# Layer 0: the last of four weights-by-values products moved into the next body, the third one's sum at the body's end

## The chip, the cores and the metric

The kernel runs on one core of a Trainium2 chip. Its engines are TensorE (PE in the profile), VectorE (DVE), ScalarE (ACT), GpSimd (POOL) and SyncE (SP), which here only issues transfers. The metric is the device time of one execution in microseconds. The kernel before took 2502.35 us, the median of three runs (2502.28 to 2506.46).

## The reference

Two transformer layers over x of 16 sequences (batches), 256 tokens, 256 features, all in float32. Layer 0, cut to what matters here:

```python
# cross attention: 16 heads of 64, causal and key mask
x1 = x + tanh(g_xattn[0]) * xattn(layernorm(x), ctx)
# "mix": attention of each token over its own 16 heads of 16
n  = layernorm(x1);  h = rmsnorm(n, gamma1)
q  = h @ Wq + bq
k, v = split((h @ Wdown + bdown) @ Wup + bup)
att = softmax(einsum('bthd,btgd->bthg', q, k) / 4)   # per token, 16 x 16
o  = einsum('bthg,btgd->bthd', att, v)
y  = n + (o @ Wo + bo)
# "moe": 8 experts, all of them, weighted by a softmax gate
h2 = rmsnorm(y, gamma2)
gate = softmax(h2 @ Wg + bg)
x2 = x1 + tanh(g_ffn[0]) * (y + sum_e gate[e] * (h2 @ We[e]))
```

Layer 1 is a cross attention with 16 heads of 16 and a feed-forward part with a shared expert and two routed ones of 1024 hidden features. The change doesn't touch it.

## The kernel before

**Staging.** Layer 0 is a pipeline over the batches. `body(a, b, c, nxt)` works on four of them at once: the attention of batch a, the mix of batch b = a - 1, the moe of batch c = a - 2, and the first projections for nxt = a + 1. In a full body all four are there: bodies 2 to 14, of which 3 to 14 are a hardware loop. Bodies 0 and 1 fill the pipeline, bodies 15, 16 and 17 empty it. Body 16 runs beside layer 1's first body and body 17 beside its second: `side_by_side` merges the programs of the two layers on each engine by the numbers that they yield. Within layer 0 alone a yielded number sets no time; the order of the code does.

**Steps.** A body has STEPS = 20 steps. In step s PE writes the scores of heads s and s + 1 (every other step), transposes the probabilities of head s - 3, and multiplies with the values five steps late. DVE takes the masked maximum of head s (`attn_max`, L745) and the reciprocal of the sum of head s - 1 (`attn_sum`, L751), ACT the exponential and the scaling. Each engine works through its instructions in order and waits on semaphores. Beside the heads lie the other stages, given to steps by tables (`mix_at`, `expert_at`, `add_at`, `score_at`, `gather_at`, L221 to L226). They share the two PSUM banks `l0_side` in one fixed order of uses. The projections of a and nxt use the two banks `l0_attn`.

**The mix of batch b.** At the start of the body DVE finishes x1 of the last batch (`attn_final`, L753; L757 and L761), takes its variance (L587 to L592) and normalises it to n (L623). Two small powers on POOL (`power`, L337) give the inverse roots. `mix_rms` (L633) makes h. PE transposes h, and projects q, down, up0 and up1 in steps 2 to 6; DVE adds the biases (L639, L645, L651). Then POOL forms the products of queries and keys, 128 x 2048 elements each, in four pieces (`query_key`, L371), and DVE sums each over its 16 features (`mix_scores`, L655). After the fourth sum comes the softmax (L662 to L672, the exponential on ACT). Then POOL forms the four products of weights and values (`weigh`, L385) and DVE sums them (`mix_gather`, L678) into o. The buffer `prod` holds two pieces: piece k + 2 waits for the sum of piece k.

**The moe of batch c.** It begins at the start of the next body: PE waits for the fourth sum, transposes o (use "oT" of the side banks), ACT and DVE split the result into a high and a low part, PE multiplies with Wo ("out"), DVE adds bias and n (`moe_residual`, L685, L688). Step 1 has `moe_squares` (L695 to L700), step 2 `moe_normalise` (L706), step 4 the transposes of h2, step 5 the gate, steps 6 to 17 the eight experts on PE and their eight weighted additions on DVE (L729). Then x2 is stored.

**For nxt**, POOL splits the context (L344, L346), DVE takes the variance of x in step 3 and normalises it to xn in step 7 (L601); PE transposes xn in step 10. POOL's `mask(a)` (L354 to L358) stands at the start of the body, and DVE waits for it before the first head.

**Transfers.** All are issued by SP in order: for each batch the loads of x (after xn_ready of the batch before), context and mask, the load of x again for the residual (after x1_copied and h_ready), and the store of x2.

Of the kernel before, what the change touches and what calls it, by code (L numbers as in the profile page):

```python
# [20 lines left out]
B, S, D = 16, 256, 256  # L21
P = 128
# [9 lines left out]
E = 8  # L32
# [134 lines left out]
def layer0(nc, ins, x2, left, right, both):  # L167
# [14 lines left out]
    xin, ctxin, xn = sb(left, "xin", [P, NT, D]), sb(left, "ctxin", [P, ND, S]), sb(left, "xn", [P, NT, D])  # L182
# [6 lines left out]
    oT = qT  # L189
# [11 lines left out]
    x1res, n, h = sb(right, "x1res", [P, NT, D]), sb(right, "n", [P, NT, D]), sb(right, "h", [P, NT, D])  # L201
# [7 lines left out]
    o, foT = h, hT  # L209
# [6 lines left out]
    for s in range(STEPS):  # L216
# [4 lines left out]
    mix_at = {2: "hT", 3: "q", 4: "down", 5: "up0", 6: "up1"}  # L221
    expert_at = {6: 0, 7: 1, 8: 2, 10: 3, 12: 4, 14: 5, 15: 6, 17: 7}
    add_at = {7: 0, 8: 1, 9: 2, 10: 3, 12: 4, 14: 5, 15: 6, 17: 7}
    score_at = {7: 0, 9: 1, 11: 2, 12: 3}

    gather_at = {15: 0, 16: 1, 18: 2, 19: 3}  # L226
# [5 lines left out]
                     ["oT", "out", "hT", "q", "down", "h2T", "up0", "gate", "up1"] + [f"we{j}" for j in range(E)] + ["idle"])  # L232
# [38 lines left out]
    def sync(sp):  # L271
        def load(b):
            if not first(b):
                sp.wait_ge(xn_ready, b)
# [40 lines left out]
        yield 17  # L315
# [6 lines left out]
    def gpsimd(pool):  # L322
# [66 lines left out]
        def body(a, b, c, nxt):  # L389
            yield BEGIN  # L390
            if a is not None:
                mask(a)
            if b is not None:
                power(varB_ready, rstdB_ready, varB, rstdB, b)
            if b is not None:
                power(ms1_ready, r1_ready, ms1, r1, b)
            if c is not None:
                power(ms2_ready, r2_ready, ms2, r2, c)
            if nxt is not None:
                split_context(nxt)  # L400
                power(varA_ready, rstdA_ready, varA, rstdA, nxt)
            if b is not None:
                yield 5.5
                query_key(b, 0, 0)
                yield 6.5
                query_key(b, 0, 1)
                yield 8.5
                query_key(b, 1, 0)
                yield 9.5
# [6 lines left out]
        power(varA_ready, rstdA_ready, varA, rstdA, 0)  # L416
        run(body(0, None, None, 1))
# [12 lines left out]
    def scalar(act):  # L430
# [68 lines left out]
        def before_exp(b, c, s):  # L499
# [7 lines left out]
            if c is not None and s == 4:  # L507
                high(side, "h2T", c, h2T[0], h2T_hi, gamma2)

        def beside_head(a, b, c, nxt, s):  # L510

            if c is not None and s == 5:
# [4 lines left out]
            if c is not None and s == 6:  # L517
# [18 lines left out]
        def body(a, b, c, nxt):  # L536
            yield BEGIN
            if c is not None:
                high(side, "oT", c, foT[0], foT_hi)
# [39 lines left out]
    def vector(dve):  # L579
# [101 lines left out]
        def moe_residual(c):  # L681
# [6 lines left out]
            V.tensor_tensor(y[:], y[:], n[:], ALU.add)  # L688
# [1217 lines left out]
```

## Time and profile before

| | |
|---|---|
| median of three runs | 2502.35 us |
| profiled execution | 2502.84 us |
| its span, first to last instruction | 2501.0 us |
| mean granted TensorE clock | 0.961 of full |
| PE busy | 2227.4 us, 89% of the span |
| DVE, ACT, POOL busy | 1480.4, 1267.7, 1023.1 us |
| layer 0 | up to about 1440 us |
| layer 1, from its first feed-forward part on | from about 1440 us |

The busy times are of one execution. PE is an average over two parts with different limits: in layer 1 it is busy nearly throughout, in layer 0 it is not, and other engines decide when it may go on. So the stretch to read is a body of layer 0, and of it who waits for whom.

### The profile page before, as it was taken

The page shows a single profiled execution, that of the slowest core. Times are in us where ns is not written, and L with a number is a line of the kernel's source. Part 1 is how long each engine was busy: PE and PEld are TensorE (multiplying, and loading weights), DVE is VectorE, ACT ScalarE, POOL GpSimd, SP SyncE. Part 2 cuts the span into 40 slices and gives each one's busy share as a digit, 9 for nine tenths or more (in the row PEclk, how much of TensorE's full clock was granted, in tenths as well). Part 3 has the DMA queues.
Part 4 walks back from the last instruction along what each step waited for, and adds up shares of the span by engine and source line. Part 5 has one row for each costly group of instructions (what it writes and reads, how often), then busy time and mean ns, then how long its engine had stood idle before and what let it go on. Part 6 is the DMA issues. An engine that isn't in the chain of part 4 may idle for free.

```text
span 2501.0 us, 47888 instructions
## 1 busy us (share of the span) xinstructions
PE 2227.4 (89%) x16000; PEld 1887.5 (75%) x16000; DVE 1480.4 (59%) x3922; ACT 1267.7 (51%) x3969; POOL 1023.1 (41%) x907
## 2 busy tenths in 40 slices
PE   5888899898888888888875799999999999999998
PEld 4667677777777777777664688888888888888888
DVE  4466666767667676676767635555555555555551
ACT  5655655556555565555633434455544444445541
POOL 1255555565555655556446213333332322333320
PEclk9999999999999999999977799999999999999999
DMA  4000000000000000000110200000000000000000
GB/s 154 8 12 14 6 17 17 17 13 4 17 17 17 13 4 17 17 17 4 39 32 13 110 16 7 13 17 17 17 17 17 17 17 16 5 13 17 17 9 9
DMA packets 26000, 51.40 MB, mean 21 GB/s; under 512 B 6160, under 2 KB 7312, under 8 KB 24784
## 3 DMA queue, kind: packets, MB, share of 16 engines
q1 hardware_dynamic: 25936, 50.57, 6.0%
q8 instruction: 37, 0.61, 0.1%
q14 instruction: 27, 0.22, 0.0%
HBM read 42.17 MB, written 8.39 MB: 20 GB/s over the span
## 4 chain that ended last, share of the span: by engine, by line
PE 57%; DVE 15%; ACT 8%; POOL 6%; issue 6%; DVEq 4%; POOLq 2%; DMA 0%; ACTq 0%
PE l_ffn L1714 13%; POOL l_prod L385 5%; PE l_ffn L161 4%; PE l_attn L161 4%; PE l_ffn L162 4%; PE l_ffn L163 4%; PE l_attn L1675 4%; PE l_attn L163 3%; PE l_attn L162 3%; DVEq L735 3%; PE l_side L161 3%; PE l_heads L1689 2%; POOLq L355 2%; PE l_side L163 2%; PE l_side L162 2%
## 5 line engine op out<-in xcount | busy, mean ns | idle before, releaser
L1253 POOL TENSOR_SCALAR l_probs<-l_probs,l_rinv 128x256 f32<-128x256 f32 x512 | 240.3, 484 | 479.2 <-DVE l_rinv L1492 478.3
L1376 ACT ACTIVATE l_probs<-l_score,l_negmax 128x256 f32<-128x256 f32 x512 | 239.1, 474 | 268.2 <-DVE l_negmax L1487 268.1
L385 POOL TENSOR_TENSOR l_prod<-l_att,l_kv 128x2048 f32<-128x2048 f32 x64 | 288.5, 4542 | 164.6 <-DVE l_att L672 164.6
L371 POOL TENSOR_TENSOR l_prod<-l_q,l_kv 128x2048 f32<-128x2048 f32 x64 | 291.2, 4561 | 150.7 <-DVE l_att L655 86.6
L1714 PE MATMUL l_ffn<-l_w,l_hid 128*128 128x256 f32 x1536 | 348.6, 381 | 1.0 <-ACT l_hid L1337 1.0
L1714 PEld LDWEIGHTS l_ffn<-l_w,l_hid 128*128 128x128 f32 x1536 | 286.2, 190 | 48.8 <-issue 12.7
L1499 DVE COPY l_probsT<-l_attn 128x512 f32<-128x512 f32 x240 | 164.5, 686 | 142.8 <-PE l_attn L1675 142.8
L745 DVE CUSTOM_DVE_ANT_0 l_probs<-l_score,l_mbias 128x256 f32<-128x256 f32 (+1 forms) x512 | 161.3, 352 | 144.9 <-PE l_score L947 95.8
L678 DVE TENSOR_REDUCE l_h<-l_prod 128x128 f32<-128x2048 f32 x64 | 146.3, 2286 | 107.5 <-POOL l_prod L385 107.2
L468 ACT ACTIVATE l_probs<-l_probs,l_negmax 128x256 f32<-128x256 f32 x256 | 130.8, 511 | 107.7 <-DVE l_negmax L745 106.6
L1487 DVE TENSOR_REDUCE l_negmax<-l_score 128x2 f32<-128x512 f32 x256 | 175.0, 684 | 15.0 <-PE l_score L1663 13.7
L485 ACT COPY l_probsT<-l_attn 128x384 f32<-128x384 f32 x256 | 120.9, 472 | 112.8 <-PE l_attn L957 112.7
L1337 ACT ACTIVATE l_hid<-l_ffn,l_b 128x256 f32<-128x256 f32 x384 | 162.1, 482 | 19.4 <-PE l_ffn L163 18.1
L1675 PE MATMUL l_attn<-l_ident,l_probs 128*128 128x128 f32 x1024 | 157.1, 279 | 11.4 <-DVE l_probsT L1499 6.6
L161 PE MATMUL l_side<-l_we_hi,l_h2T_hi 128*128 128x256 f32 x512 | 159.8, 312 | 2.2 <-DVE l_acc L729 1.8
L161 PE MATMUL l_attn<-l_cT_hi,l_wk_hi 128*128 128x256 f32 x384 | 124.0, 323 | 40.6 <-DVE l_xT_lo L609 39.0
L655 DVE TENSOR_REDUCE l_att<-l_prod 128x128 f32<-128x2048 f32 x64 | 145.8, 2279 | 5.0 <-issue 4.4
L162 PE MATMUL l_side<-l_we_lo,l_h2T_hi 128*128 128x256 f32 x512 | 147.5, 288 | 0.0
L163 PE MATMUL l_side<-l_we_hi,l_h2T_lo 128*128 128x256 f32 x512 | 147.1, 287 | 0.0
L476 ACT ACTIVATE l_probs<-l_probs,l_rinv 128x256 f32<-128x256 f32 x256 | 127.6, 498 | 24.3 <-DVE l_rinv L751 24.3
L1675 PEld LDWEIGHTS l_attn<-l_ident,l_probs 128*128 128x128 f32 x1024 | 118.8, 143 | 25.4 <-issue 12.4
L1238 POOL TENSOR_TENSOR l_rstdF<-l_varF,l_neghalf 128x2 f32<-128x2 f32 x16 | 11.2, 701 | 303.1 <-DVE l_varF L1421 303.1
(261 smaller groups left out, 7177.2 us busy)
## 6 DMA issues: line engine op xcount, KB each, us to landing
l_ctxin<-in_ctx SPq DMA_DIRECT2D x32, 256.0 KB, 3.0
l_xin<-in_x SPq DMA_DIRECT2D x16, 256.0 KB, 2.6
l_x<-in_x SPq DMA_DIRECT2D x16, 256.0 KB, 2.6
x<-l_acc SPq DMA_DIRECT2D x16, 256.0 KB, 2.0
l_xin<-x SPq DMA_DIRECT2D x16, 256.0 KB, 3.1
l_x<-x SPq DMA_DIRECT2D x16, 256.0 KB, 2.6
out<-l_x SPq DMA_DIRECT2D x16, 256.0 KB, 2.0
l_hid<-in_w SPq DMA_DIRECT2D x2, 1536.0 KB, 8.2
```

The lines of the kernel that those rows point to most:

```text
L161: last = nc.tensor.matmul(out, wh, xh, start=n == 0, stop=False)
L162: last = nc.tensor.matmul(out, wh, xl, start=False, stop=False)
L163: last = nc.tensor.matmul(out, wl, xh, start=False, stop=n == len(terms) - 1)
L371: nc.gpsimd.tensor_tensor(prod[:, u].rearrange("p (h g d) -> p h g d", h=half, g=H), q4[:, u * half:(u + 1) * half].unsqueeze(2).to_broadc ...
L385: nc.gpsimd.tensor_tensor(prod[:, u].rearrange("p (h d g) -> p h d g", h=half, d=HD), a4.unsqueeze(2).to_broadcast([P, half, HD, H]), v4.u ...
L1253: last = nc.gpsimd.tensor_scalar(probs[:, j % 4, t * S:(t + 1) * S], probs[:, j % 4, t * S:(t + 1) * S], rinv[:, j, t:t + 1], 1.0, ALU.mul ...
L1337: last = nc.scalar.activation(hid[:, c, :], ps[:, u * S:(u + 1) * S], ACT.Relu, bias=b1[:, c:c + 1])
L1376: last = nc.scalar.activation(probs[:, s % 4, t * S:(t + 1) * S], ps[:, t * S:(t + 1) * S], ACT.Exp, bias=negmax[:, s, t:t + 1], accum_out ...
L1487: V.tensor_reduce(negmax[:, j], ps[:].rearrange("p (t k) -> p t k", t=NT), axis=AX.X, op=ALU.max, negate=True).then_inc(max_ready, 1)
L1499: V.tensor_copy(probsT[:, j % RING, :], ps[:]).then_inc(free, 1)
L1675: last = T.transpose(ps[:, kt * S + t * P:kt * S + (t + 1) * P], probs[:, j % 4, t * S + kt * P:t * S + (kt + 1) * P], ident[:])
L1714: last = T.matmul(ps[:, 0:D], hid[:, c, t * P:(t + 1) * P], w2[:, c, :], start=c == 0, stop=c == 3 * NHC - 1)
```

## The change

The fourth product `weigh(b, 3)` moves from the end of a body into the next one, where the batch is called c: on POOL behind the two powers of the start, ahead of the split of the context. Its sum, `mix_gather(c, 3)`, is done by DVE in step 2 of that body; the third sum is done at the end of the body, ahead of `attn_final`. What follows the sums moves with them: oT to step 3, out to step 4, squares to 5, normalise to 6, h2T to 7, gate to 8, experts to steps 9 to 18. The mix's projections move by one step (3 to 7), the first score sum from step 7 to 8. xn moves from step 7 to 8, the variance of x from 3 to 4. `mask` is done for the next batch, between the second and third product. As n and h are overwritten before c has used them, n is copied to a new buffer `nres`, and o and its transpose lie in the buffers of y and h2T; the copies of n and x1 stand in step 9. xn shares the buffer of xin, so that x is loaded only after xn's transpose was copied out.

```diff
-    xin, ctxin, xn = ... sb(left, "xn", [P, NT, D])
+    xin, ctxin = ...
-    oT = qT
+    xn, oT = xin, qT
...
-    o, foT = h, hT
+    o, foT = y, h2T
...
-    mix_at = {2: "hT", 3: "q", 4: "down", 5: "up0", 6: "up1"}
-    expert_at = {6: 0, 7: 1, 8: 2, 10: 3, 12: 4, 14: 5, 15: 6, 17: 7}
-    add_at = {7: 0, 8: 1, 9: 2, 10: 3, 12: 4, 14: 5, 15: 6, 17: 7}
-    score_at = {7: 0, 9: 1, 11: 2, 12: 3}
-
-    gather_at = {15: 0, 16: 1, 18: 2, 19: 3}
+    mix_at = {3: "hT", 4: "q", 5: "down", 6: "up0", 7: "up1"}
+    moe_at = {3: "oT", 4: "out", 7: "h2T", 8: "gate"}
+    expert_at = {9: 0, 10: 1, 11: 2, 13: 3, 14: 4, 16: 5, 17: 6, 18: 7}
+    add_at = {10: 0, 11: 1, 12: 2, 14: 3, 15: 4, 17: 5, 18: 6, 19: 7}
+    score_at = {8: 0, 9: 1, 11: 2, 12: 3}
+
+    gather_at = {16: 0, 18: 1}
...
-                     ["oT", "out", "hT", "q", "down", "h2T", "up0", "gate", "up1"] + [f"we{j}" for j in range(E)] + ["idle"])
+                     ["hT", "oT", "q", "out", "down", "up0", "up1", "h2T", "gate"] + [f"we{j}" for j in range(E)] + ["idle"])
...  SP
-                sp.wait_ge(xn_ready, b)
+                sp.wait_ge(xT_hi, b)
             sp.dma_start(xin[:], ins["x"][bass.ds(b, 1)][0]).then_inc(x_in, 16)
...  POOL
             yield BEGIN
-            if a is not None:
-                mask(a)
             if b is not None:
                 power(varB_ready, rstdB_ready, varB, rstdB, b)
-            if b is not None:
                 power(ms1_ready, r1_ready, ms1, r1, b)
+            yield 0.5
             if c is not None:
-                power(ms2_ready, r2_ready, ms2, r2, c)
+                weigh(c, 3)
+            yield 3.2
             if nxt is not None:
                 split_context(nxt)
                 power(varA_ready, rstdA_ready, varA, rstdA, nxt)
+            yield 5.2
+            if c is not None:
+                power(ms2_ready, r2_ready, ms2, r2, c)
             if b is not None:
...
-                for piece in range(4):
-                    yield 13.5 + piece
-                    weigh(b, piece)
+                yield 13.8
+                weigh(b, 0)
+                yield 15
+                weigh(b, 1)
+            yield 15.9
+            if nxt is not None:
+                mask(nxt)
+            if b is not None:
+                yield 16.5
+                weigh(b, 2)
...  DVE, moe_residual
-            V.tensor_tensor(y[:], y[:], n[:], ALU.add)
+            V.tensor_tensor(y[:], y[:], nres[:], ALU.add)
...  DVE, beside_head
-            if s == 0 and b is not None:
+            if s == 1 and b is not None:
                 mix_rms(b)
-            if s == 1:
-                if c is not None:
-                    moe_squares(c)
-                if b is not None:
-                    V.tensor_copy(x1res[:], x1[:]).then_inc(x1_copied, 1)
+            if s == 2 and c is not None:
+                mix_gather(c, 3)
...
+            if s == 9 and b is not None:
+                V.tensor_copy(nres[:], n[:])
+                V.tensor_copy(x1res[:], x1[:]).then_inc(x1_copied, 1)
             if nxt is not None:
-                if s == 3:
+                if s == 4:
                     pre_variance(nxt)
-                elif s == 7:
+                elif s == 8:
                     pre_normalise(nxt)
...  DVE, body
             yield STEPS
+            if b is not None:
+                mix_gather(b, 2)
             if a is not None:
                 attn_final(a)
...  PE, beside_head
+                use = moe_at.get(s)
+                if use == "oT":
+                    pe.wait_ge(gathered, 4 * (c + 1))
+                    transpose4(side, "oT", c, o)
+                elif use == "out":
+                    side.emptied(pe, "oT", c)
+                    tokens(side, "out", c, foT, fo, D)
```

In `beside_head` of DVE and PE the projections of b come ahead of the moe stages of c in the same step, those ahead of the copies, the copies ahead of the stages of nxt, and the score sums come last.

## Rows read from the trace of the kernel before

**Rows 1.** Windows: length, busy time of each engine (instructions), clock, DMA share, GB/s.
```profile
790.00:868.38 78.38, 68.70 (x490) 56.86 (x489) 54.60 (x155) 45.46 (x142) 42.58 (x18) 0.98 0.04 14
...
850.00:869.00 19.00, 16.27 (x102) 13.00 (x100) 11.66 (x21) 8.51 (x24) 18.77 (x6) 1.00 0.13 41
```

**Rows 2.** Chain of waits, in order of time: start us, us, what.
```profile
765.09 2.29 DVE l_att L655
...
793.01 0.12 PE l_attn L163
...
843.46 2.29 DVE l_att L655
...
868.04 2.30 DVE l_h L678
```

**Rows 3.** Timeline of POOL, one body: start us, us, instructions, idle before.
```profile
799.99 0.69 POOL L337 TENSOR_TENSOR l_r<-l_ms,l_neghalf 128x2 f32<-128x2 f32 x1 [3.68 <-DVE l_ms L627]
803.67 0.80 POOL L337 TENSOR_TENSOR l_r<-l_ms,l_neghalf 128x2 f32<-128x2 f32 x1 [2.99 <-DVE l_ms L700]
...
814.33 9.10 POOL L371 TENSOR_TENSOR l_prod<-l_q,l_kv 128x2048 f32<-128x2048 f32 x2 [3.92 <-DVE l_kv L651]
827.44 4.60 POOL L371 TENSOR_TENSOR l_prod<-l_q,l_kv 128x2048 f32<-128x2048 f32 x1 [4.02 <-DVE l_att L655]
833.29 4.52 POOL L371 TENSOR_TENSOR l_prod<-l_q,l_kv 128x2048 f32<-128x2048 f32 x1 [1.25 <-DVE l_att L655]
849.97 18.04 POOL L385 TENSOR_TENSOR l_prod<-l_att,l_kv 128x2048 f32<-128x2048 f32 x4 [12.16 <-DVE l_att L672]
868.09 0.41 POOL L354 TENSOR_SCALAR l_mbias<-l_maskbits 128x256 f32<-128x256 uint8 x1
...
869.25 0.72 POOL L358 TENSOR_TENSOR l_mbias<-l_cmask,l_mbias 128x256 f32<-128x256 f32 x1
```

**Rows 4.** Timeline of PE, one body.
```profile
784.81 5.77 PE L980 MATMUL l_attn<-l_wo,l_qT 128*128 128x256 f32 x26
...
836.72 0.39 PE L161 MATMUL l_attn<-l_cT_hi,l_wk_hi 128*128 128x256 f32 x1 [2.48 <-DVE l_xT_lo L609]
837.06 0.28 PE L163 MATMUL l_attn<-l_cT_hi,l_wk_lo 128*128 128x256 f32 x1
...
837.67 0.42 PE L161 MATMUL l_attn<-l_cT_hi,l_wk_hi 128*128 128x256 f32 x1
...
861.88 7.07 PE L980 MATMUL l_attn<-l_wo,l_qT 128*128 128x256 f32 x32
870.48 0.65 PE L879 MATMUL l_side<-l_ident,l_h 128*128 128x128 f32 x4 [1.53 <-DVE l_h L678]
```

**Rows 5.** Timeline of DVE, one body.
```profile
791.89 0.68 DVE L757 TENSOR_TENSOR l_ytmp<-l_attn,l_bo 128x512 f32<-128x512 f32 x1
...
797.07 0.69 DVE L685 TENSOR_TENSOR l_y<-l_side,l_bfo 128x512 f32<-128x512 f32 x1 [1.54 <-PE l_side L163]
...
800.10 0.42 DVE L745 CUSTOM_DVE_ANT_0 l_probs<-l_score,l_mbias 128x256 f32<-128x256 f32 x1 [0.18 <-issue]
...
800.72 0.61 DVE L633 TENSOR_SCALAR l_h<-l_n,l_r 128x256 f32<-128x256 f32 x2
...
824.43 0.74 DVE L601 TENSOR_SCALAR l_xn<-l_xin,l_mvA,l_rstdA 128x256 f32<-128x256 f32 x2
```

**Rows 6.** Timeline of DVE: body 0, and the copy of x1 in a full body.
```profile
119.28 3.97 DVE L601 TENSOR_SCALAR l_xn<-l_xin,l_mvA,l_rstdA 128x256 f32<-128x256 f32 x2
...
803.50 0.42 DVE L772 COPY l_x1res<-l_x 128x512 f32<-128x512 f32 x1
```

**Rows 7.** Timeline of POOL in body 0.
```profile
113.74 9.03 POOL L371 TENSOR_TENSOR l_prod<-l_q,l_kv 128x2048 f32<-128x2048 f32 x2 [3.33 <-DVE l_kv L651]
```

More of the change, by code:

```diff
@@ L181, in layer0 @@
     maskbits, cmask = sb(left, "maskbits", [P, S], U8), sb(left, "cmask", [P, CAUSAL])
-    xin, ctxin, xn = sb(left, "xin", [P, NT, D]), sb(left, "ctxin", [P, ND, S]), sb(left, "xn", [P, NT, D])
+    xin, ctxin = sb(left, "xin", [P, NT, D]), sb(left, "ctxin", [P, ND, S])
     statA, mvA, varA, rstdA = sb(left, "statA", [P, NT, 6]), sb(left, "mvA", [P, NT, 2]), sb(left, "varA", [P, NT]), sb(left, "rstdA", [P, NT])
@@ L200, in layer0 @@
     x1, ytmp = sb(right, "x1", [P, NT, D]), sb(right, "ytmp", [P, NT, D])
-    x1res, n, h = sb(right, "x1res", [P, NT, D]), sb(right, "n", [P, NT, D]), sb(right, "h", [P, NT, D])
+    x1res, nres, n, h = sb(right, "x1res", [P, NT, D]), sb(right, "nres", [P, NT, D]), sb(right, "n", [P, NT, D]), sb(right, "h", [P, NT, D])
     statB, mvB, varB, rstdB = sb(right, "statB", [P, NT, 6]), sb(right, "mvB", [P, NT, 2]), sb(right, "varB", [P, NT]), sb(right, "rstdB", [P, NT])
@@ L314, in sync @@
         load_residual(B - 1)
-        yield 17
+        yield 19.6
         store(B - 3)
@@ L506, in before_exp @@
                 nc.scalar.activation(dT[0][:], ps[0:LAT, 0:S], ACT.Identity, bias=bdown[:]).then_inc(dT_hi, 1)
-            if c is not None and s == 4:
+            if c is not None and moe_at.get(s) == "oT":
+                high(side, "oT", c, foT[0], foT_hi)
+            if c is not None and moe_at.get(s) == "h2T":
                 high(side, "h2T", c, h2T[0], h2T_hi, gamma2)
         def beside_head(a, b, c, nxt, s):
-            if c is not None and s == 5:
+            if c is not None and s == 8:
                 act.wait_ge(glog_ready, c + 1)
@@ L516, in beside_head @@
                 last.then_inc(gexp_done, 1)
-            if c is not None and s == 6:
+            if c is not None and s == 9:
                 act.wait_ge(gsum_ready, c + 1)
@@ L823, in body @@
             yield BEGIN
-            if c is not None:
-                low(side, "oT", c, foT, foT_hi)
             if b is not None:
@@ L829, in body @@
             yield BEGIN_OUT
-            if c is not None:
-                moe_residual(c)
             if b is not None:
@@ L1011, in beside_head @@
             if c is not None:
-                if s == 4:
+                use = moe_at.get(s)
+                if use == "oT":
+                    pe.wait_ge(gathered, 4 * (c + 1))
+                    transpose4(side, "oT", c, o)
+                elif use == "out":
+                    side.emptied(pe, "oT", c)
+                    tokens(side, "out", c, foT, fo, D)
+                elif use == "h2T":
                     pe.wait_ge(h2_ready, c + 1)
                     transpose4(side, "h2T", c, y)
-                elif s == 5:
+                elif use == "gate":
                     side.emptied(pe, "h2T", c)
@@ L1022, in body @@
             yield BEGIN
-            if c is not None:
-                pe.wait_ge(gathered, 4 * (c + 1))
-                transpose4(side, "oT", c, o)
             if a is not None:
@@ L1030, in body @@
             yield BEGIN_OUT
-            if c is not None:
-                side.emptied(pe, "oT", c)
-                tokens(side, "out", c, foT, fo, D)
             if a is not None:
```

23 lines of the change are left out of this document (13 added, 10 removed).

## The prediction

> **What bounds the kernel now.** The windows of equal length come first: a body of layer 0 lasts 78.4 us, and in the one from 790.00 PE is busy 68.70, DVE 54.60, POOL 42.58 [rows 1]. No engine is full, so the time is set by waits. The chain of waits shows which: its piece for the fourth score sum returns after 843.46 - 765.09 = 78.37 us [rows 2], the body's period. In each body the chain goes through the per-token attention of the batch before: softmax, then POOL's four products of weights and values, 18.04 us in one piece from 849.97 [rows 3], then the last sum at 868.04 [rows 2], and the oT transposes, before which PE sat idle for 1.53 us [rows 4].
>
> I cut the period at three points, all in the body from PE's end of attn_out, 784.81 + 5.77 = 790.58 (called E), to its next end, 861.88 + 7.07 = 868.95 [rows 4].
> Front, E to the first query-key product: 814.33 - 790.58 = 23.75.
> Middle, from there to the first weigh product: 849.97 - 814.33 = 35.64.
> Back, from there to the next E: 868.95 - 849.97 = 18.98. Sum 78.37.
>
> **The change, part by part.**
>
> *Back: the fourth product and sum leave, mask(nxt) enters.* POOL then needs 3 x 4.51 = 13.5 us and the mask 869.97 - 868.09 = 1.9 [rows 3], then one sum of 2.3 [rows 2]: 17.7 us after softmax. PE's own work ends at 18.98, so PE becomes last here. It also gets one expert more behind the softmax (four instead of three): 12 matmuls of 0.12 us [rows 2], 1.4 us. PE had 19.00 - 16.27 = 2.73 us idle there [rows 1], partly because the second sum stood ahead of the last head's reciprocal, which it no longer does; I let 1.1 of the 1.4 fall into that idle time. Back after: 19.3 (bounds 18.0 and 20.4).
> The 1.53 us stall at the oT transposes goes, but it lay at the start of the front and is counted there.
>
> *Front: no oT and out at its start, but weigh(c,3) and gather(3) in it.* Between attn_final and the first head's maximum DVE took 800.10 - 791.89 = 8.2 us [rows 5]. Without the oT subtraction (about 0.8) and without the wait for out and the residual (about 2.3, around 797.07) it is 5.1, so E + 5.2. POOL's power for ms1 starts when that maximum does and takes 0.69 [rows 3]; weigh(c,3) is right behind it on POOL and runs from about E + 5.9 to E + 10.4. On DVE mix_rms, the h pass, comes at about E + 7.2. It is a tensor_scalar from SBUF to SBUF, and what such an instruction does beside a POOL product is shown in body 0: L601, 0.74 us for two when alone at 824.43, took 3.97 from 119.28, until POOL's pair of products begun at 113.74 (9.03 long) was over [rows 5 to 7]. So mix_rms ends at about E + 11.1, head 2's maximum at 11.8, gather(3) at 14.0. Only then may PE transpose oT, for which it waits some 2.2 us in step 3.
> Behind that wait stand on PE, in order: the transposes (0.65), q2, scores, q and out (3 x 12 matmuls of 0.12 us and the scores' 8 in 0.9, 5.2 us): E + 19.9. DVE cannot go on to the residual before. Then come, on DVE, residual 1.45, variance 1.4, two heads 1.5, dT 0.45, squares 1.7 and kv 0.65, in sum 7.1 (estimates from the spacing of the same instructions between 792 and 820): the first query-key product starts at E + 26.9. Front after: 26.9 against 23.75, +3.2. Lower bound 24.5 (mix_rms slips in ahead of the product, gather right behind it, 0.7 + 1.7 less), upper 28.5 (TensorE's clock falls in step 3: in rows 4 the matmuls behind an idle 2.48 us are at 0.42 instead of 0.28, that is 1.2 instead of 2.4 GHz, and this costs some 1.6 us a time).
>
> *Middle: xn one step later, the two residual copies in step 9, first score sum in step 8.* Query-key 0 and 1 take 9.10 us [rows 3]. Before, xn (824.43) came 1.0 us after they were over (823.43) and met an idle POOL. After, DVE reaches step 8 sooner after the first product, because gate, oT and out are spread out: at about 5.3 us, in the middle of the second product. By the row of body 0 it then stands until 9.15, and the sum follows at 9.9, done at 12.1. That sum releases query-key 2 on POOL (4.60 [rows 3]). In step 9 DVE does one maximum and two reciprocals, 0.7 us, and comes to the copies nres and x1res. A copy alone takes 0.42 [rows 6]. No row shows a copy behind a POOL product, so it is bounded: 2 x 0.36 = 0.7 if nothing holds it, 3.9 + 0.7 if the product does. I take the latter: the copy has the same form, SBUF to SBUF, as the held tensor_scalar, and the pow on POOL that started 0.17 us behind it took 0.80 instead of 0.69 [rows 3, 6, 7]. So: product over at 16.7, copies 17.5, second sum 19.7. Then steps 10 to 12 on DVE: 1.5, 2.0 for xT, 1.5 + 2.2, 1.6 gives the fourth sum at 28.6, and from it to the first weigh product it is as before 849.97 - 843.46 = 6.5. Middle after: 35.1 against 35.64, -0.5. Lower bound 28.6 (neither xn nor the copies held), upper 37 (see the clock rival).
>
> The Trainium skill, "SBUF — State Buffer", section "Who interferes with whom", says that VectorE's copies and tensor_scalars in their two-port modes, and instructions with two SBUF inputs, lock each other out with GpSimd for the whole instruction, whichever issues first. L601 in body 0 agrees; for copies, only the pow at 0.80 points that way. By the rule the copies are held and the body is 81.3; were they free, the same sum gives 77.5.
>
> *Added and dropped besides.* One copy of 0.42 (nres), counted. The load of x now waits for xT_hi (step 11) instead of xn_ready (step 7), and is queued on SP behind the store of step 19 in either kernel: its 2.6 us are awaited only in step 4 of the next body, some 20 us later, so it costs nothing. x1_copied moves from step 1 to 9, and load_residual with it; attn_final needs it over 35 us later. mask no longer stands at the body's start; it now lies between weigh 1 and 2, counted. split_context comes behind weigh(c,3), 4.5 us later, needed in step 9: nothing.
>
> *Sum.* 26.9 + 35.1 + 19.3 = 81.3, that is +2.9 a body. Bodies that have all three batches and a next one: 2 to 14, 13 of them: +38 us. Body 1 has no c: about -1. Bodies 15 and 16 each end sooner (their last POOL product was in the chain, 4.5 us) and pay the front, about -1 each; in the last one weigh(15,3), its sum and everything up to x2 of batch 15 come one to two steps later, and the load of w1 waits for x2: +3. The ends together 0 (bounds -10 and +8). The profiled execution took 2502.84 (span 2501.0), 0.5 above the median: 2502.84 + 38 - 0.5 = 2540.
>
> **Rivals.**
> *Faster (30%).* DVE is not held, at least not by query-key 2, and PE's order sets the time. For it: the POOL chain that ends the body does get shorter than PE, 17.7 against 18.98; PE is idle 9.7 us of 78.4 now [rows 1], and the early steps lose a 1.53 us stall and gain work in their gaps. Against: body 0's 3.97. With copies free the middle is 31.3 and the body 77.5, -0.9; with xn free too it is 28.6 and 75, -3.4. Over 13 bodies -12 to -44, middle -28: 2474.
> *No change (8%).* The oT wait only moves from the body's start to step 3, and the rest cancels: 2502. For it: 1.53 goes and about 2.2 come.
> *Slower by the clock as well (15%).* With DVE late in steps 8 to 10, PE has done what it may and waits for add 0 in step 11, some 9 us. At a 2.48 us gap the clock already fell to half for what followed [rows 4]; after a longer one k1 and the scores of step 12 run at 1.2 GHz, on the chain. Price 1.5 to 3 us a body more: 13 x 5 = 65, 2567.
> *The forecast (47%)*: 2540, its own range 2525 to 2556.
>
> **How the numbers follow.** About 0.2%, 5 us, is what a measurement can tell from no change. Slower: 47 + 15 = 62%; within: 8%; faster: 30%. The ends of the range: up to 2570, past the middle of the clock case; down to 2470, past the middle of the faster case; some 18% is left outside. The sides are far apart because one question, whether a POOL product holds a DVE copy, carries 3.8 us of every body.
>
> **What would show it.** In the changed profile: period of the score sums near 81 (right) or under 78 (wrong). L633 near 3.9 us for its pair instead of 0.61 [rows 5], right beside a POOL L385; L601 stretched to the end of query-key 1; the copies at about 4 us together. gather(3) ending some 14 us after attn_out and the oT transposes idle before it by 2 us. First query-key product 27 us after attn_out, the first weigh 62. The body's end on PE's attn_out with DVE waiting for PE. If the copies keep 0.42, the middle is wrong and the kernel is faster. If the front stays under 24.5, the walk through out and the residual is wrong.

## The result and the profile after

The changed kernel took 2646.89 us, the median of four runs (2645.70 to 2648.15). The kernel before, run on the same chip, took 2504.40 (2502.28 to 2507.33). The ratio is 1.057, with an interval of 1.055 to 1.0586. The forecast of 2540 had the direction and missed the size: +38 us were expected, +142 came, and the time lies above the range.

Of the page, the first part. DVE is busy 1660.8 us against 1480.4 before. The change adds one copy of 0.42 us to a batch, so almost all of these 180 us are instructions that lasted longer.

```profile
span 2645.6 us, 47941 instructions
...
PE 2272.3 (86%) x16000; PEld 1932.3 (73%) x16000; DVE 1660.8 (63%) x3938; ACT 1269.6 (48%) x3969; POOL 1022.0 (39%) x907
```

How long is a body now? The last products with Wo mark its end. First the kernel before, ends of body 1 and of body 14, then the same two after, with the end of body 8 between them, from which E = 784.50 comes (timeline of PE: start us, us).

```profile
155.33 7.07 PE L980 MATMUL l_attn<-l_wo,l_qT 128*128 128x256 f32 x32
...
1178.45 7.07 PE L980 MATMUL l_attn<-l_wo,l_qT 128*128 128x256 f32 x32
```

```profile
162.30 7.07 PE L996 MATMUL l_attn<-l_wo,l_qT 128*128 128x256 f32 x32
...
777.43 7.07 PE L996 MATMUL l_attn<-l_wo,l_qT 128*128 128x256 f32 x32
...
1303.43 7.07 PE L996 MATMUL l_attn<-l_wo,l_qT 128*128 128x256 f32 x32
```

Bodies 2 to 14 took 1023.12 us before and 1141.13 after: +118.0, or +9.1 each. The spans differ by 2645.6 - 2501.0 = 144.6, so 26.6 came outside these 13 bodies.

The windows answer to [rows 1]: the body from E = 784.50 to 872.79, cut at the same three points as in the prediction. Columns: length, busy time of PE, PEld, DVE, ACT and POOL (instructions), clock, DMA share, GB/s.

```profile
784.50:814.63 30.13, 25.76 (x168) 21.22 (x167) 22.10 (x69) 16.68 (x52) 9.18 (x7) 0.89 0.00 0
814.63:852.96 38.33, 30.43 (x198) 25.16 (x198) 31.31 (x63) 20.52 (x68) 18.15 (x4) 0.82 0.02 7
852.96:872.79 19.83, 18.64 (x124) 16.06 (x125) 12.46 (x24) 8.55 (x24) 15.26 (x6) 1.00 0.12 41
784.50:872.79 88.29, 74.83 (x490) 62.44 (x490) 65.87 (x155) 45.75 (x142) 42.59 (x17) 0.88 0.04 12
```

One body stands here for 13. Their means, after against before: front 29.5 against 23.2, middle 38.4 against 36.0, back 19.8 against 19.5.

| | before | forecast | after |
|---|---|---|---|
| front | 23.75 | 26.9 | 30.13 |
| middle | 35.64 | 35.1 | 38.33 |
| back | 18.98 | 19.3 | 19.83 |
| body | 78.37 | 81.3 | 88.29 |

I call an instruction held when it stands until a POOL product is over. DVE's timeline of this body answers to [rows 5, 6]. The two h instructions have 4.09 instead of 0.61 us, the two of `moe_normalise` (L717) 4.82, the first residual copy 4.32, while the second has 0.41 and xn 0.73.

```profile
791.64 4.09 DVE L644 TENSOR_SCALAR l_h<-l_n,l_r 128x256 f32<-128x256 f32 x2
...
796.28 2.26 DVE L689 TENSOR_REDUCE l_y<-l_prod 128x128 f32<-128x2048 f32 x1
...
814.47 4.82 DVE L717 TENSOR_SCALAR l_y<-l_y,l_r 128x256 f32<-128x256 f32 x2
...
824.34 0.42 DVE L756 CUSTOM_DVE_ANT_0 l_probs<-l_score,l_mbias 128x256 f32<-128x256 f32 x1 [2.10 <-PE l_score L963]
...
826.84 0.17 DVE L723 TENSOR_TENSOR l_glog<-l_side,l_bg 128x16 f32<-128x16 f32 x1 [1.78 <-PE l_side L163]
...
827.20 0.73 DVE L612 TENSOR_SCALAR l_xin<-l_xin,l_mvA,l_rstdA 128x256 f32<-128x256 f32 x2
827.84 2.28 DVE L666 TENSOR_REDUCE l_att<-l_prod 128x128 f32<-128x2048 f32 x1
...
830.73 4.32 DVE L810 COPY l_nres<-l_n 128x512 f32<-128x512 f32 x1
834.97 0.41 DVE L811 COPY l_x1res<-l_x 128x512 f32<-128x512 f32 x1
```

Now POOL, answering to [rows 3]. Lay the two beside each other: each long DVE instruction or pair is over soon after a POOL product ends. 790.40 + 4.56 = 794.96 lies inside the h pair, which is over 0.8 us later; 814.63 + 4.5 = 819.1 is the end of the first query-key product, and L717 ends at 819.29; 830.20 + 4.56 = 834.76, and L810 ends at 835.05.

```profile
790.40 4.56 POOL L386 TENSOR_TENSOR l_prod<-l_att,l_kv 128x2048 f32<-128x2048 f32 x1
...
814.63 9.02 POOL L372 TENSOR_TENSOR l_prod<-l_q,l_kv 128x2048 f32<-128x2048 f32 x2 [0.72 <-DVE l_kv L662]
...
830.20 4.56 POOL L372 TENSOR_TENSOR l_prod<-l_q,l_kv 128x2048 f32<-128x2048 f32 x1 [6.54 <-DVE l_att L666]
...
852.96 9.18 POOL L386 TENSOR_TENSOR l_prod<-l_att,l_kv 128x2048 f32<-128x2048 f32 x2 [10.74 <-DVE l_att L683]
```

PE's timeline answers to [rows 4]. Twice PE waits for a held stage, 2.07 us for gather(3) and 5.39 for L717. Behind the first wait the products of q2 last 0.41 us instead of 0.28, which is how they look at 1.2 instead of 2.4 GHz.

```profile
798.60 1.11 PE L895 MATMUL l_side<-l_ident,l_y 128*128 128x128 f32 x4 [2.07 <-DVE l_y L689]
...
799.94 0.41 PE L163 MATMUL l_attn<-l_xT_hi,l_wq_lo 128*128 128x256 f32 x1
...
819.34 0.90 PE L895 MATMUL l_side<-l_ident,l_y 128*128 128x128 f32 x3 [5.39 <-DVE l_y L717]
```

Behind the second wait the clock stays at 0.50 for longer, 13.5 us (window of this stretch), and in it DVE waits for PE: 2.10 us for scores and 1.78 for the gate, in the rows above.

```profile
818.00:831.50 13.50, 12.16 (x57) 10.12 (x59) 8.66 (x26) 6.68 (x23) 6.96 (x3) 0.50 0.00 0
```

The chain of waits goes through the same places: L717 and the copy L810 are pieces of it.

```profile
796.36 2.19 DVE l_y L689
...
814.73 4.57 DVE l_y L717
819.34 1.11 PE l_side L895 x4
...
830.81 3.71 DVE l_nres L810
```

### The profile page after: what moved, and what is told of

Its sections match the earlier page's. It is cut to its first block, busy times and chain, and to the rows that moved or that the text cites. A ratio compares the mean times of both kernels' runs of the same rounds, so it can differ in the third digit from the quotient of the medians.

```text
span 2645.6 us, 47941 instructions
## 1 busy us (share of the span) xinstructions
PE 2272.3 (86%) x16000; PEld 1932.3 (73%) x16000; DVE 1660.8 (63%) x3938; ACT 1269.6 (48%) x3969; POOL 1022.0 (39%) x907
## 4 chain that ended last, share of the span: by engine, by line
PE 60%; DVE 20%; issue 9%; ACT 4%; DVEq 3%; POOL 2%; DMA 1%; POOLq 0%; ACTq 0%; SPq 0%
PE l_ffn L1731 13%; PE l_ffn L161 4%; PE l_attn L996 4%; PE l_ffn L162 3%; PE l_ffn L163 3%; PE l_attn L1692 3%; PE l_attn L161 3%; PE l_side L161 3%; PE l_attn L162 3%; PE l_attn L163 3%; DVE l_y L717 3%; PE l_heads L1706 2%; DVE l_att L666 2%; PE l_side L163 2%; PE l_side L162 2%
## 5 line engine op out<-in xcount | busy, mean ns | idle before, releaser
L161 PE MATMUL l_side<-l_we_hi,l_h2T_hi 128*128 128x256 f32 x512 | 166.9, 326 | 65.1 <-DVE l_acc L740 64.9
L689 DVE TENSOR_REDUCE l_y<-l_prod 128x128 f32<-128x2048 f32 x64 | 145.9, 2279 | 60.9 <-POOL l_prod L386 60.5
L1504 DVE TENSOR_REDUCE l_negmax<-l_score 128x2 f32<-128x512 f32 x256 | 175.1, 684 | 12.2 <-PE l_score L1680 10.8
L1354 ACT ACTIVATE l_hid<-l_ffn,l_b 128x256 f32<-128x256 f32 x384 | 162.1, 482 | 20.4 <-PE l_ffn L163 19.3
L161 PEld LDWEIGHTS l_side<-l_we_hi,l_h2T_hi 128*128 128x128 f32 x512 | 107.2, 209 | 79.7 <-DVE l_acc L740 74.6
L163 PE MATMUL l_side<-l_we_hi,l_h2T_lo 128*128 128x256 f32 x512 | 154.8, 302 | 0.0
L162 PE MATMUL l_side<-l_we_lo,l_h2T_hi 128*128 128x256 f32 x512 | 154.8, 302 | 0.0
L895 PE MATMUL l_side<-l_ident,l_y 128*128 128x128 f32 x128 | 34.4, 421 | 118.1 <-DVE l_y L717 74.3
```

Source lines behind the costliest of these rows:

```text
L161: last = nc.tensor.matmul(out, wh, xh, start=n == 0, stop=False)
L162: last = nc.tensor.matmul(out, wh, xl, start=False, stop=False)
L163: last = nc.tensor.matmul(out, wl, xh, start=False, stop=n == len(terms) - 1)
L1504: V.tensor_reduce(negmax[:, j], ps[:].rearrange("p (t k) -> p t k", t=NT), axis=AX.X, op=ALU.max, negate=True).then_inc(max_ready, 1)
```

## The experiments

My theory was: a copy or tensor_scalar from SBUF to SBUF on VectorE stands still while a GpSimd product runs; the change brought three of these into products, and TensorE, waiting for them, lost clock besides. The rivals were the new order of the steps as such, and the clock alone. Twelve kernels ran, four at a time, each time beside the kernel before.

| kernel | median us | ratio to before | interval |
|---|---|---|---|
| weigh3_first | 2576.55 | 1.030 | 1.0282 to 1.0317 |
| normalise_first | 2610.08 | 1.0434 | 1.0417 to 1.0452 |
| copies_step5 | 2572.85 | 1.0282 | 1.0264 to 1.0299 |
| all_out_of_products | 2486.36 | 0.9935 | 0.9918 to 0.9952 |
| fillers_at_waits | 2613.57 | 1.0453 | 1.0436 to 1.0471 |
| before_copy_step9 | 2568.09 | 1.0275 | 1.0257 to 1.0292 |
| weigh_norm_copies | 2481.17 | 0.9922 | 0.9905 to 0.9938 |
| all_out_and_filler | 2431.63 | 0.972 | 0.9704 to 0.9737 |
| copies_as_reductions | 2573.64 | 1.0302 | 1.028 to 1.0324 |
| three_moved_filler | 2478.87 | 0.9909 | 0.9893 to 0.9926 |
| all_out_filler_red | 2427.43 | 0.9712 | 0.9696 to 0.9728 |
| before_filler | 2496.92 | 0.9984 | 0.9975 to 0.9994 |

The kernel before had medians of 2501.30, 2499.49 and 2502.01 in the three groups of four.

Rows of the form "L810 DVE ..." below are the view that groups instructions by line, of 400 to 1000 us: busy us and mean ns of one, then idle time before. Line numbers shift by one or two between kernels. Distances such as "the second sum 20.7 us after the first product" are differences of starts in the timelines of POOL and DVE.

**weigh3_first.** On GpSimd the fourth product stands first in the body.

```diff
             yield BEGIN
+            if c is not None:
+                weigh(c, 3)
             if b is not None:
                 power(varB_ready, rstdB_ready, varB, rstdB, b)
                 power(ms1_ready, r1_ready, ms1, r1, b)
-            yield 0.5
-            if c is not None:
-                weigh(c, 3)
```

> The changed kernel with one edit on GpSimd: weigh(c,3) is the first thing in the body, right behind weigh(c,2) of the body before, instead of behind the two powers. Theory (a VectorE instruction with SBUF in and SBUF out stands still as long as a GpSimd product runs): the product is over about 0.3 us after attn_out, before VectorE comes to mix_rms; mix_rms falls from a mean of 2.09 us to about 0.37 us an instruction, gather(3) needs no wait, oT is transposed at about 11 us after attn_out instead of 14.1, TensorE does not fall to 1.2 GHz there. Front 30.1 -> 24.2 us, middle and back as in the changed kernel, body 82.4, 13 bodies x -5.9 = -77: about 2570 us. Rival 1 (the steps' new order on TensorE and VectorE sets the time, the held mix_rms is hidden): within 10 us of 2647. Rival 2 (the clock): mix_rms short but TensorE's clock falls all the same, about 2600.

Measured 2576.55, -70 against the changed kernel. The h instruction is back at 341 ns.

```profile
L643 DVE TENSOR_SCALAR l_h<-l_n,l_r 128x256 f32<-128x256 f32 x14 | 4.2, 341 | 0.0
```

The front of a body and its clock (window from E, and the middle behind it):

```profile
754.97:779.70 24.73, 23.23 (x168) 19.00 (x167) 18.73 (x69) 16.37 (x52) 4.94 (x8) 1.00 0.00 0
779.70:817.59 37.89, 27.78 (x198) 23.25 (x198) 31.47 (x63) 20.28 (x68) 18.20 (x4) 0.86 0.03 7
```

The front falls from 30.13 to 24.73 with clock 1.00, the middle stays: as expected. The new order of the steps, with the fourth sum in it, costs the front 1 us against the 23.75 of before, not 6.

**normalise_first.** On VectorE `moe_normalise(c)` moves ahead of `mix_kv(b, 0)` in step 6.

```diff
+            if c is not None and s == 6:
+                moe_normalise(c)
             if b is not None and s in mix_at:
...
-                elif s == 6:
-                    moe_normalise(c)
```

> The changed kernel with one edit on VectorE: in step 6 moe_normalise(c) stands ahead of mix_kv(b,0), whose end releases the first query-key product. Theory (held by the product): moe_normalise falls from 4.8 us a pair to about 0.75, the first product starts 0.75 us later, xn in step 8 now falls into the second product and is held instead, the first score sum 2.5 to 3.3 us earlier after the product. Body -2.5 us (bounds -1 and -4), 13 x -2.5 = -33: about 2614 us. Rival (moe_normalise waits for GpSimd's power r2 or is hidden behind TensorE's work): +0.7 a body, 2655.

Measured 2610.08, -37. The expected exchange is there: L717 is free, and xn (L612), which was not held in the changed kernel, now is.

```profile
L612 DVE TENSOR_SCALAR l_xin<-l_xin,l_mvA,l_rstdA 128x256 f32<-128x256 f32 x14 | 27.7, 2019 | 0.0
...
L717 DVE TENSOR_SCALAR l_y<-l_y,l_r 128x256 f32<-128x256 f32 x14 | 4.3, 350 | 0.0
```

**copies_step5.** The two residual copies in step 5.

```diff
-            if s == 9 and b is not None:
+            if s == 5 and b is not None:
                 V.tensor_copy(nres[:], n[:])
                 V.tensor_copy(x1res[:], x1[:]).then_inc(x1_copied, 1)
```

> The changed kernel with one edit on VectorE: the copies nres and x1res in step 5, behind moe_squares(c), instead of step 9. Theory (held by query-key 2): the nres copy falls from 4.3 us to about 0.4, the front grows by 0.8, the second score sum starts 4.5 us earlier, but the fourth product waits for the third to end, so the middle shrinks by 2.8 only: body -2.0 us, 13 x -2.0 = -26: about 2621 us. Rival (the copies are hidden behind TensorE or the product anyway): +0.8 a body, 2657.

Measured 2572.85, -74: nearly three times what I expected.

```profile
L810 DVE COPY l_nres<-l_n 128x512 f32<-128x512 f32 x7 | 2.9, 419 | 0.0
```

The step of the expectation that failed is "the fourth product waits for the third to end". The third sum follows the second by 8.3 us here and by 7.3 in the changed kernel. That is VectorE's and TensorE's own work of steps 10 and 11, and POOL's product fits into it. So all of the 4.3 us was on the path: ten of the 13 bodies have a middle of 32.8 to 33.3 instead of 37.7 to 39.2. The other three (each fourth one) have 33.7 and last 87 us: their back is 22.6 instead of 19.8, and the clock falls in it too (0.57 from 727.21 to 735.21).

**all_out_of_products.** The three edits together, and xn in step 6 ahead of `mix_kv(b, 0)`.

```diff
+            if nxt is not None and s == 6:
+                pre_normalise(nxt)
...
-                elif s == 8:
-                    pre_normalise(nxt)
```

> The changed kernel with all three edits (weigh(c,3) first, moe_normalise ahead of mix_kv(b,0), copies in step 5) and xn in step 6 ahead of mix_kv(b,0) instead of step 8, so that no VectorE instruction of these meets a GpSimd product. Theory: front 24.2 + 2.3 = 26.5, middle 28.6 to 31, back 19.3: body 74.4 to 77, that is -11 to -14 us against the changed kernel, about 2470 to 2500 us: faster than the kernel before, or level with it. Rival (the order of steps itself costs): the body stays above 80, over 2540 us.

Measured 2486.36: below the kernel before. But its bodies, with nothing held, are not alike. From body 4 on their lengths go round between 74.4, 77.2, 79.0 and 80.1 us; here are two that follow each other:

```profile
707.15:781.53 74.38, 67.97 (x490) 56.52 (x490) 54.44 (x155) 45.11 (x142) 42.31 (x17) 0.98 0.04 15
781.53:860.55 79.02, 72.58 (x491) 60.48 (x490) 54.56 (x155) 45.57 (x142) 42.83 (x18) 0.91 0.04 14
```

The instructions are the same in both. In both PE is idle for 2.4 us ahead of the h2T transposes (it waits for `mix_kv` 0 to free its bank), and in both the clock falls behind that gap. They differ in how long it stays down: some 3.4 us in the short body, some 11 in the long one, whose clock falls a second time in its back (0.67 from 841.53 to 844.53). First the gap in the long body, then the stretch at the low clock in either:

```profile
807.98 0.63 PE L894 MATMUL l_side<-l_ident,l_y 128*128 128x128 f32 x4 [2.40 <-DVE l_kv L661]
...
734.30:737.70 3.40, 3.40 (x20) 2.03 (x17) 1.23 (x3) 2.67 (x9) 3.40 (x1) 0.50 0.00 0
808.50:819.50 11.00, 11.00 (x58) 8.96 (x56) 7.22 (x18) 7.32 (x27) 10.96 (x3) 0.54 0.00 0
```

**fillers_at_waits.** The changed kernel, with products on TensorE whose result is overwritten.

```diff
+        def filler(use, c, count):
+            ps, full, free, turn = side.at(use, c)
+            pe.wait_ge(free, turn)
+            for _ in range(count):
+                T.matmul(ps[:, 0:S], we[0][:, 0, 0:P], we[0][:, 0, 0:S], start=True, stop=True)
...
                 if use == "oT":
+                    filler("oT", c, 16)
...
                 elif use == "h2T":
+                    filler("h2T", c, 44)
```

> The changed kernel, nothing moved; TensorE gets products whose result is overwritten, just ahead of its two long waits: 16 of 128x256 ahead of the oT transposes (step 3) and 44 ahead of the h2T transposes (step 7), 0.12 us each, so they lie inside the 2.1 and 5.4 us of idle time. Every hold of VectorE stays. It prices the clock. My theory: the holds are the larger part, the clock takes what runs at 1.2 GHz behind the two waits, about 2.2 us in the front and 1.5 to 2 in the middle: body -4, 13 x -4 = -52, about 2595 us (bounds 2580 and 2625). Rival 1 (the clock is all of it): near 2500. Rival 2 (the clock costs nothing on the path): 2647.

```profile
765.15:792.72 27.57, 25.12 (x186) 20.92 (x184) 22.02 (x69) 16.57 (x52) 9.21 (x7) 1.00 0.00 0
792.72:830.43 37.71, 32.33 (x242) 27.88 (x242) 31.62 (x63) 20.25 (x68) 18.39 (x5) 0.91 0.02 7
```

Measured 2613.57, -33, inside the bounds that I had set. The front's clock is 1.00 instead of 0.89 and its length 27.57 instead of 30.13; the middle gains only 0.6. The holds are unchanged (L717 and L810 at 2534 and 4339 ns). But this does not leave all the rest to them. The fillers moved the low clock of the middle, they did not remove it: the first sum now comes 10.4 us after the first product instead of 13.2, and then PE waits 4.45 us for DVE's first addition of an expert (2.17 in the changed kernel), with the clock at 0.50 behind it.

```profile
813.00:819.50 6.50, 5.15 (x24) 4.12 (x25) 4.97 (x16) 2.66 (x9) 4.53 (x1) 0.50 0.00 0
...
814.35 0.58 PE L161 MATMUL l_side<-l_we_hi,l_h2T_hi 128*128 128x256 f32 x1 [4.45 <-DVE l_acc L740]
```

So the clock costs at least 33 of the 142 us; how the rest divides between the holds and the clock behind them is open.

**before_copy_step9.** In the kernel before, its one copy moves from step 1 to step 9, into a product.

```diff
             if s == 1:
                 if c is not None:
                     moe_squares(c)
-                if b is not None:
-                    V.tensor_copy(x1res[:], x1[:]).then_inc(x1_copied, 1)
+            if s == 9 and b is not None:
+                V.tensor_copy(x1res[:], x1[:]).then_inc(x1_copied, 1)
```

> The kernel BEFORE with one edit: its copy x1res moved from step 1 to step 9 on VectorE, where it is issued some 2.5 us after query-key 2 has begun on GpSimd (in the trace of before, 829.9 against 827.44). Nothing else moves. Theory (a copy is held until the product is over): the copy lasts about 2.1 us instead of 0.42, the second score sum comes 2.1 us later and query-key 3 with it; body +2, over 14 bodies +28: about 2530 us. Rival (only the new order of steps makes a copy slow, or the delay is absorbed by TensorE's waits): within 6 us of 2502.

```profile
L772 DVE COPY l_x1res<-l_x 128x512 f32<-128x512 f32 x7 | 16.9, 2409 | 0.0
```

Measured 2568.09, +69. The hold is as expected (2.41 us against 2.1), the price is more than twice the expected 28: the 13 bodies last 82.8 us on average instead of 78.7. Where the first sum stands as before, the second is 2.3 us later and the fourth 3.1, and in some bodies the clock falls already beside the first two products. Two stretches of the same work in two bodies, from the first product to the first sum:

```profile
519.95:530.80 10.85, 10.82 (x89) 9.02 (x90) 4.16 (x19) 7.28 (x28) 9.10 (x2) 1.00 0.00 0
...
601.48:615.30 13.82, 13.79 (x89) 11.29 (x90) 4.05 (x18) 7.28 (x28) 9.01 (x2) 0.77 0.00 0
```

This puts one of the suspected causes by itself into a kernel that has nothing else of the change.

**weigh_norm_copies.** all_out_of_products without the move of xn.

> As all_out_of_products, but xn stays in step 8. Theory: VectorE comes to xn while the second query-key product runs and is held until it is over, 9.1 us after the first began; xn's mean rises from 0.41 us to about 1.7 to 2, the front is 0.7 shorter (25.6), the first score sum at 9.9 instead of 6.1 to 6.8, middle 31 to 34.5. Body +2 to +3 against all_out_of_products: 2512 to 2525 us. Rival (xn's place does not matter): 2477 to 2490.

```profile
L611 DVE TENSOR_SCALAR l_xin<-l_xin,l_mvA,l_rstdA 128x256 f32<-128x256 f32 x16 | 30.3, 1931 | 0.0
```

Measured 2481.17, a miss: xn is held as expected, but the kernel is no slower than with xn moved (2486.36). Its bodies between 397 and 1092 us are 75.4 to 78.3 long and its mean clock is 0.955, against 74.4 to 80.1 and 0.948. The freed xn gained nothing, and the clock is the likely taker; the next kernel tests that by keeping it up.

**all_out_and_filler.** all_out_of_products with 16 products ahead of the second up product.

```diff
             ps, full, free, turn = side.at(f"up{t}", b)
             pe.wait_ge(free, turn)
+            for _ in range(16 * t):
+                T.matmul(ps[:, 0:S], fq[0][:, 0, 0:P], fo[0][:, 0, 0:S], start=True, stop=True)
```

> all_out_of_products with 16 products of 128x256 (overwritten) on TensorE ahead of the second up product in step 7, 1.9 us, so that the 2.4 us of idle time before the h2T transposes shrink to 0.5. In all_out_of_products every second body went at 1.2 GHz behind that gap (79 to 80 us a body against 74.4). Theory (the gap makes the clock fall): all bodies 74.4 to 75, 13 x -2.8 = -36 against 2486: about 2450 us. Rival (the clock falls for another reason, or the filler delays kv1): 2486 or more.

```profile
674.44:700.79 26.35, 25.14 (x185) 20.94 (x183) 20.49 (x75) 17.33 (x55) 5.05 (x7) 1.00 0.03 10
700.79:727.61 26.82, 24.76 (x198) 20.71 (x198) 21.53 (x57) 19.28 (x64) 18.20 (x4) 1.00 0.00 0
727.61:747.44 19.83, 18.64 (x124) 16.08 (x125) 12.46 (x24) 8.54 (x24) 19.46 (x7) 1.00 0.12 41
674.44:747.44 73.00, 68.54 (x507) 57.73 (x506) 54.47 (x155) 45.14 (x142) 42.71 (x18) 1.00 0.05 15
```

Measured 2431.63, 2.8% below the kernel before, and 19 below my expectation. The body shown is 73.0, at full clock in all three parts; one in four lasts 74.5, with the clock down in its back, and the mean of the 13 is 73.4 against 77.7 without the filler.

**copies_as_reductions.** The changed kernel; the copies stay in step 9 and change their form.

```diff
-                V.tensor_copy(nres[:], n[:])
-                V.tensor_copy(x1res[:], x1[:]).then_inc(x1_copied, 1)
+                V.tensor_reduce(nres[:].rearrange("p t n -> p (t n)"), n[:].rearrange("p t (n o) -> p (t n) o", o=1),
+                                axis=AX.X, op=ALU.add)
+                V.tensor_reduce(x1res[:].rearrange("p t n -> p (t n)"), x1[:].rearrange("p t (n o) -> p (t n) o", o=1),
+                                axis=AX.X, op=ALU.add).then_inc(x1_copied, 1)
```

> The changed kernel with the two copies left in step 9, at the very same place behind query-key 2, but written as another form: tensor_reduce over an axis of length one, which gives the same values. It tells the place from the form. Theory (only forms such as copy and tensor_scalar from SBUF to SBUF are held; the sums beside products kept 2.29 us in every trace): each lasts 0.4 to 0.8 us instead of 4.3 and 0.41, the second score sum starts 3 to 4 us earlier after query-key 2, middle about 34.5; body -4, 13 x -4 = -52 and the clock as in copies_step5: 2570 to 2600 us. Rival (whatever VectorE issues there waits for the product, a semaphore or the drain): no change, 2647.

```profile
L812 DVE TENSOR_REDUCE l_x1res<-l_x 128x512 f32<-128x512 f32 x7 | 4.7, 676 | 0.0
L810 DVE TENSOR_REDUCE l_nres<-l_n 128x512 f32<-128x512 f32 x7 | 4.7, 666 | 0.0
```

Measured 2573.64, the same as with the copies moved away. Same place, same product beside it, 0.67 us instead of 4.32: it is the form of the instruction that is held, not its place in the order. The Trainium skill, "SBUF — State Buffer", section "Who interferes with whom", says that on trn2 a reduction never contends with GpSimd while a copy can; the trace agrees, with these 0.67 and 4.32 us.

**three_moved_filler.** weigh_norm_copies with the filler, to size xn's hold.

> weigh_norm_copies (weigh(c,3) first, moe_normalise ahead of mix_kv(b,0), copies in step 5, xn still held in step 8) with the filler of all_out_and_filler on TensorE. It sizes the held xn with the clock kept up. Theory: xn about 2 us an instruction, the first score sum 9.4 us after the first query-key product instead of 4.6, but the second product (over at 9.1) is what the second sum waits for anyway, so the later sums come 3.1 us later, the front is 0.7 shorter: body 75.4 against 73.4, 13 x 2.0 to 2.4: 2457 to 2463 us. Rival (xn's hold hidden behind the product): 2422 to 2435.

```profile
L611 DVE TENSOR_SCALAR l_xin<-l_xin,l_mvA,l_rstdA 128x256 f32<-128x256 f32 x16 | 39.4, 2501 | 0.0
```

Measured 2478.87. Against all_out_and_filler the one held xn costs 47 us (expected 26 to 31): the first sum comes 9.5 us after the first product instead of 4.6, the fourth 4 to 5 us later. It is not the hold alone. Behind it PE waits 3.31 us ahead of the xT transposes and the clock falls to 0.50 there, and the mean clock is 0.963 against 0.974.

**all_out_filler_red.** all_out_and_filler with the copies as reductions in step 9.

> A candidate: all_out_and_filler with the copies as reductions in step 9 instead of copies in step 5. Theory: 0.84 us leave the front; in step 9 the two reductions (0.7 us each) lie partly in VectorE's idle time before the second product ends. Body 73.4 -> 72.4 to 73.2: 2418 to 2430 us. Rival (the reductions are held after all, or lie on the path): 2440 or more.

Measured 2427.43. Its ratio, 0.9712, lies inside the interval of all_out_and_filler, so the two can't be told apart.

**before_filler.** The kernel before, with 16 such products ahead of the head transposes of step 11.

> The kernel BEFORE with 16 products of 128x256 (overwritten) on TensorE ahead of the head transposes of step 11, 1.9 us inside the 2.48 us gap behind which its clock fell. It tells how much of the best kernel's gain is the filler's alone. Theory: the first products of k1 and what follows in step 12 run at 2.4 instead of 1.2 GHz, 1.6 us a body if on the path: 13 x -1.6 = -21, about 2480 us (bounds 2470 and 2502). Rival (the filler delays the head transposes and with them the body): 2505 to 2520.

Measured 2496.92, ratio 0.9984. It was a miss: the mean clock stayed 0.961 and most bodies stayed at 78.4. The filler did its work at its own place: in the body from 867.59 the clock stays 1.00 there and the fourth sum follows the third by 4.8 us instead of 6.3. But the clock now falls beside the first two products (0.66 over the 5 us from 891.33), and the first sum comes 12.3 us after the first product instead of 10.8. At this place, then, a filler alone brings 0.2%. No other place was tried in the kernel before, so how much of the 2.8% it could have by fillers alone is open.

## Why the prediction was wrong in its size

**What held.** That a product holds a copy or tensor_scalar, and the front up to the oT transposes: gather(3) ends at 796.28 + 2.26 = 798.54, 14.04 us after E, as forecast (14.0). The oT wait is 2.07 us (2.2). The copies took 4.32 + 0.41 us where I had chosen 3.9 + 0.7, and the product ends them as said. The back is 19.8 against 19.3. The changes of transfers and the mask cost nothing that shows.

**The step that failed: "at about 5.3 us, in the middle of the second product", in the middle part.** VectorE was to reach step 8 there, with only xn held. This walk let `moe_normalise` pass at its old duration. In the changed kernel it stands right behind `mix_kv(b, 0)`, whose end releases the first query-key product. The product began 0.16 us after the pair did, and VectorE stood until 819.29. TensorE, waiting for it, went on at half the clock, and VectorE then waited for TensorE. So the walk reached xn at 12.6 us after the first product (827.20 - 814.63), not 5.3. xn then met an idle GpSimd, so one hold replaced the other; the first sum started at 13.2 instead of 9.9. From there each time is the forecast one plus 3.2 us: second sum 20.7 (17.5), fourth 31.8 (28.6). (In the other bodies the first sum starts at 11.6 to 13.2, the fourth at 31.1 to 32.7.)

Two runs part the hold from the clock. fillers_at_waits has the same hold with the clock up, and the first sum starts at 10.4 there: in the body shown, 2.8 of the 3.3 us came by way of the clock. normalise_first gives the case that I had described, without that hold: xn held at 2.02 us, the sum at 9.5 and the middle at 35.7 to 37.0, on average 36.2, where I forecast 35.1 and the changed kernel has 38.4. So leaving out this hold, with the clock behind it, cost the forecast 2.3 us a body.

**A term left in the bounds that belonged in the sum: the clock.** In step 3 I had named it as the front's upper bound, with 1.6 us. The transposes of h and of oT are all that PE has between 794.7 and 799.4, and the clock falls there. fillers_at_waits prices it at 30.13 - 27.57 = 2.6 us of the front's 3.2 in the body shown, and at 29.5 - 27.6 = 2.0 on average. In the middle the clock was a rival with 15%, by a wait for add 0 in step 11 of some 9 us. In the changed kernel that wait is 2.17 us and the clock is 1.00 behind it; the long wait there is the one of 5.39 us that the hold made. But where the first sum comes early, the wait that I had named is there, at half its length and with the clock at 0.50 behind it: 4.45 us in fillers_at_waits, 4.63 in normalise_first. In normalise_first the third sum is on time (24.2, forecast 24.7), and behind this wait the fourth is not (29.2 to 30.5, forecast 28.6).

```profile
820.49 0.58 PE L161 MATMUL l_side<-l_we_hi,l_h2T_hi 128*128 128x256 f32 x1 [4.63 <-DVE l_acc L740]
```

**Bodies outside the 13.** I set them at 0, with bounds of -10 and +8; it was +26.6. Body 1 went from 67.42 to 73.48 (forecast -1), body 15 from 76.70 to 85.01 (forecast -1), and from the last attn_out to the end the kernel takes 1250.1 instead of 1238.8 us. Body 1 has no c, so neither weigh(c,3) nor `moe_normalise`; it has the copies and xn, and the runs separate them. It lasts 69.3 us with the copies in step 5 (copies_step5), 69.2 in weigh_norm_copies and 65.7 once xn is moved too (all_out_of_products). So the held copies cost it 4.1 us and the held xn 3.5, more than the 6.1 that it grew by. Body 15 falls from 85.0 to 82.1 in weigh3_first and in normalise_first, to 79.1 in copies_step5, and to 72.1 with nothing held.

**The sum.** 13 x 2.9 was forecast; 13 x 9.1 + 27 came. The medians say the same without windows: against 2646.9 the three held stages are worth 70, 37 and 74 us one at a time and 166 together (weigh_norm_copies), more than the whole loss of 142. These prices hold the clock that goes down behind each. Without them the changed kernel is 0.8% faster than the one before.

**The rivals.** "Faster" had the condition that VectorE is not held, and that was false in the kernel as changed. Its sum was near: it gave 2474, and 2486.36 and 2481.17 were measured once nothing, or only xn, was held. That is partly luck, as these kernels have another order and lose clock besides; with the clock up it is 2431.63. "No change" fell with the result. That the order of the steps as such costs the time is refuted by weigh3_first and weigh_norm_copies. "Slower by the clock as well", 2567, came nearest of the four and was still 80 us too low; in the body shown the clock did fall, twice, but not at the wait in step 11 from which this rival had its price.

## What to carry to other kernels

When instructions of VectorE move past the start of a GpSimd product, walk every SBUF-to-SBUF copy and tensor_scalar of that stretch, not only those that the change names; above all the one right behind the instruction that releases the product. Put it ahead of the release, or give it a form that isn't held: here 0.67 us as a reduction instead of 4.32 as a copy. A hold costs more than its length where TensorE waits for it and loses clock behind the wait: a copy that took 2.41 us instead of 0.42 lengthened the bodies of the kernel before from 78.7 to 82.8 us on average, 4.1 each. So judge such an edit only with the clock in view, and look for the stretch at 0.50 in the whole body: in fillers_at_waits and before_filler it left the place that was filled and came back at another.

## What the runs showed of the hardware that I had not expected

- GpSimd gets in between two VectorE instructions of one pair: L717 began at 814.47 and the product at 814.63, and the pair ended only behind the product. Being issued 0.16 us earlier protected at most the first of the two.
- Behind the same gap of 2.4 us on PE, with the same instructions, the clock stays at 0.50 for some 3.4 us in one body and some 11 in the next: 74.4 and 79.0 us, clock 0.98 and 0.91. Why the lengths differ no run shows. 16 overwritten products, 1.9 us, in that gap brought all three parts of the body shown to 1.00 and the kernel from 2486.36 to 2431.63.
- VectorE's additions with one input from SBUF and one from PSUM were not held: `mix_kv` 1 took 0.67 us at 819.84, beside the second product.
